# A fused Mamba and soft mixture-of-experts kernel: tables that place the second output projection, the x_proj product, both silus, GpSimd's w products and ScalarE's convolution inputs

## The chip, the cores and the metric

The kernel runs on one core of one Trainium2 chip. The metric is the device time of one execution in microseconds (us). The kernel before takes 7782.45 us, the median of three runs (7781.32 to 7786.65).

## The reference, cut to what matters

The input is one sequence of 8192 rows of width 512. It goes through a two-layer Mamba block with a residual, and then through a soft mixture of experts with a residual. The change touches the Mamba layers alone. Each of the two layers computes:

```
xz = x @ W_in.T;  xc, z = split(xz)                    # 512 -> 2 x 1024 channels
u = silu(causal_conv(xc, 4 taps) + b_c)
dt, Bm, Cm = split(u @ W_x.T, [32, 48])                # x_proj: 1024 -> 64
delta = softplus(dt @ W_dt.T + b_dt)
h_t = exp(delta_t * A) * h_{t-1} + delta_t * Bm_t * u_t   # 16 states for each of 1024 channels
y_t = sum over states of h_t * Cm_t + u_t * D
out = (y * silu(z)) @ W_out.T                          # 1024 -> 512
```

Everything is float32. The recurrence over 8192 rows cannot be cut along the sequence, so the kernel walks along it.

## The kernel before

**Tiling.** A layer is cut into 16 chunks of 512 rows; with two layers, 32 chunks run one after the other. A chunk has 128 slots: 32 groups (16 states, for each of two halves of the channels) times four blocks of 128 channels. The first half's states fill slots 0 to 63, the second half's 64 to 127. VectorE runs one scan (`h`, L1289) for two slots, so a chunk has 64 scans, at the even slots.

**What the engines do in a slot.** ScalarE computes the factor exp(delta * A) of the scan (`decay`, L928), for two slots at every even slot, and the scan reads it; the ring `decay` holds four slots, so ScalarE may run one scan ahead of VectorE. GpSimd multiplies `w` by the row of B (`bu`, L1172), one instruction for each scan, up to three scans ahead. TensorE transposes a finished state back, 128 rows at a time (`turn`, L666, one tile in every slot), and VectorE multiplies it by C and adds it up (`acc`, L1317 for the first of a half, L1319 for the others); one tile of four goes to ScalarE instead (`prod`, L958), and GpSimd adds those (`prod`, L1214, and `acc`, L1223). There are two `turn` banks, so the transposes of a slot wait until the tile of two slots before has been read. ScalarE's tiles of `prod` lie at the slots that leave 6 or 7 when divided by 8; at slots 4 and 12, and so on, VectorE's scan therefore follows the one before at once, with no `acc` between.

**The work beside the scan.** Between its transposes TensorE runs the projections of the neighbouring chunks: `conv_half` (the product with the first half of W_in), `conv` (the four taps, as products with diagonal matrices), `x_proj`, `turn_c` (C transposed), `delta` and `delta_next` (the product with W_dt), `gate` (the second half of W_in), `out` (the product with W_out) and, in the first 14 chunks of layer 0, `norm` (the transposes of the rows of the chunk after the next). Each ends in one of two `proj` banks (`RING = 2`), in turn, so a product waits until the tile two before it in the list has been taken.

**What sets the order.** The list `ORDER` names these tiles in order, and `timetable()` spreads their products over the slots by weights. ScalarE takes a finished tile `TAKE_LAG` slots after its last product, corrected by `TAKE_LATER`: it copies it out of the bank, and for `out`, `norm` and `x_proj` it issues the DMA that stores it. Within a slot ScalarE first runs the factors of the scan (at even slots), then its `prod`, then the takes. For `conv_half` a take is the copy into `conv_in` and `halo` (L815 to L818); the diagonal matrices (`taps`, L808) are made `TAPS_LEAD` slots earlier. `SILU_LATER` says how many slots after a take the silu of four blocks follows (`u`, L829, and `zy`, L871): the silu needs another table of functions, so two table loads go with it. `W_AT` and `HEAD_AT` say before which scan's input GpSimd runs the sum and the product that make the next `w` (L1154 and L1161), and the small instructions for the first column of a chunk (L1181 and L1191 to L1200).

All engines run in order and wait for each other through semaphores. After the two layers three short stages compute the mixture of experts (L1418 on); they are not touched.

Of the kernel before, what the change touches and what calls it, by code (L numbers as in the profile page):

```python
# [40 lines left out]
ORDER = [('conv_half', 0, 0), ('conv_half', 1, 0), ('delta', 4, 0), ('conv', 0, 8), ('conv_half', 2, 0), ('delta',  # L41
         5, 0), ('conv', 1, 0), ('conv_half', 3, 0), ('delta', 6, 0), ('conv', 2, 0), ('delta', 7, 0), ('conv_half',
         4, 0), ('conv', 3, 0), ('conv_half', 5, 0), ('conv', 4, 0), ('conv_half', 6, 0), ('conv', 5, 0),
         ('conv_half', 7, 0), ('conv', 6, 0), ('conv', 7, 0), ('norm', 0, 0), ('out', 0, 0), ('norm', 1, 8), ('norm', 2, 0),
         ('x_proj', 0, 0), ('norm', 3, 0), ('turn_c', 0, 0), ('out', 1, 0), ('delta_next', 0, 0),
         ('delta_next', 1, 0), ('out', 2, 0), ('delta_next', 2, 0), ('delta_next', 3, 4), ('out', 3, 0), ('gate', 0,
         4), ('gate', 1, 0), ('gate', 2, 0), ('gate', 3, 0), ('gate', 4, 0), ('gate', 5, 0), ('gate', 6, 0),
         ('gate', 7, 0)]
# [1 line left out]
SLOTS_BODY = GROUPS * HB  # L50
PAIRS = SLOTS_BODY // 2
TAKE_LAG, TAPS_LEAD, XDBL_LAG, CONV_LAG, PROD_LAG = 3, 2, 3, 3, 2
TAKE_LATER = {('out', 0): -1, ('gate', 0): 1, ('gate', 2): 2, ('delta_next', 0): -1, ('conv', 5): -1, ('delta', 5): -1}
SILU_LATER = (4, 4, 1, 1)
V_SUM_AT = (10, 10, 10, 10, 10, 10, 10, 9, 9, 9, 10, 10, 10, 10, 10, 9)
JOIN_AT = (41, 72)

W_AT = {13: ('sum', 2), 16: ('product', 2), 20: ('sum', 3), 23: ('product', 3), 47: ('sum_next', 0), 51:
        ('product_next', 0), 55: ('sum_next', 1), 59: ('product_next', 1)}

HEAD_AT = {24: ('exponent', 1), 28: ('state', 1), 56: ('exponent_next', 0), 61: ('state_next', 0)}
HEAD_EXP_AT = {51: ('exp', 1), 117: ('exp_next', 0)}
BFIRST_AT = 24

# [51 lines left out]
def timetable():  # L116
# [5 lines left out]
    for i, (kind, x, earliest) in enumerate(ORDER):  # L122
        if kind == "conv":
            earliest = max(earliest, end_of["conv_half", x] + CONV_LAG + TAKE_LATER.get(("conv_half", x), 0))
        if kind == "x_proj":
            earliest = end_of["conv", NB - 1] + TAKE_LATER.get(("conv", NB - 1), 0) + TAKE_LAG + SILU_LATER[1] + 4
        if kind in ("turn_c", "delta_next"):
            earliest = end_of["x_proj", 0] + XDBL_LAG + TAKE_LATER.get(("x_proj", 0), 0)
        slots = []
# [9 lines left out]
        end = end_of[kind, x] = slots[-1]  # L139
        late = end + TAKE_LAG + TAKE_LATER.get((kind, x), 0)  # L140
        if kind == "conv_half":
# [5 lines left out]
        if kind == "conv" and x % HB == HB - 1:  # L147
            take[late + SILU_LATER[x // HB]].append(("silu_u", x // HB, i))
        if kind == "gate" and x % HB == HB - 1:
            take[late + SILU_LATER[2 + x // HB]].append(("silu_z", x // HB, i))  # L150
    return work, take, end_of
# [142 lines left out]
def mamba_stack(nc, ctx, d, rstd, nmr):  # L294
# [828 lines left out]
    def _(pool):  # L1123
# [17 lines left out]
        def bias(X):  # L1141

            pool.wait_ge(norm_step, X * 11 + 11)
            rows = slice(X * J, X * J + J)
            pool.tensor_tensor(nmr[:, rows], neg_mean[:], rstd[:, rows], ALU.mult).then_inc(bias_set, 1)
# [91 lines left out]
        def body(G, kind):  # L1237
            for p in range(PAIRS):
                what, pair = W_AT.get(p, ("", 0))
                if what and kind.has(what.replace("sum", "delta").replace("product", "delta")):  # L1240
                    delta_w(G, what, pair)
                if p == BIAS_AT and kind.norms:
                    bias(G + NORM_AHEAD)
                if p in HEAD_AT:
                    what, hf = HEAD_AT[p]
                    X = G + what.endswith("_next")
# [906 lines left out]
```

## Time and profile before

| | |
|---|---|
| median of three runs | 7782.45 us (7781.32 to 7786.65) |
| the profiled execution | 7782.23 us, its span 7780.4 us |
| TensorE, matmuls | 7040.2 us busy, 90% of the span |
| VectorE | 7073.6 us, 91% |
| ScalarE | 6030.5 us, 78% |
| GpSimd | 6668.8 us, 86% |
| mean granted TensorE clock | 0.974 of full speed |
| VectorE's 2048 scans | the first starts 99.2 us after the span's start, the last at 7197.5 us |

A share of busy time is an average over the whole span. The two Mamba layers fill it up to the last scan; what follows belongs to the mixture of experts, in which GpSimd has little to do. In a view of the timeline, the time in brackets at the end of a row is how long the engine stood idle before that row, and what is named behind the arrow is what ended that idle time. The view of the waits adds such idle times up by pairs of waiter and releaser. PE is TensorE, DVE VectorE, ACT ScalarE, POOL GpSimd and SP the queue of DMA issues.

### The profile page before, as it was taken

The page shows a single profiled execution, that of the slowest core. Times are in us where ns is not written, and L with a number is a line of the kernel's source. Part 1 is how long each engine was busy: PE and PEld are TensorE (multiplying, and loading weights), DVE is VectorE, ACT ScalarE, POOL GpSimd, SP SyncE. Part 2 cuts the span into 40 slices and gives each one's busy share as a digit, 9 for nine tenths or more (in the row PEclk, how much of TensorE's full clock was granted, in tenths as well). Part 3 has the DMA queues.
Part 4 walks back from the last instruction along what each step waited for, and adds up shares of the span by engine and source line. Part 5 has one row for each costly group of instructions (what it writes and reads, how often), then busy time and mean ns, then how long its engine had stood idle before and what let it go on. Part 6 is the DMA issues. An engine that isn't in the chain of part 4 may idle for free. (4 is left out here: it accounts for less than half of the span.)

```text
span 7780.4 us, 98947 instructions
## 1 busy us (share of the span) xinstructions
PE 7040.2 (90%) x29580; PEld 3887.5 (50%) x29580; DVE 7073.6 (91%) x6228; ACT 6030.5 (78%) x13267; POOL 6668.8 (86%) x3115
## 2 busy tenths in 40 slices
PE   7899999999999999999999999999999999987799
PEld 3454554554454545544444445444444454444664
DVE  5999999999999999999999999999999999999655
ACT  7888888888878888877777788777777787776564
POOL 5999999999999999999999999999999999998010
PEclk9899999999999999999999999999999999998899
DMA  3222222222222222222222222222222222221665
GB/s 107 76 85 86 79 86 77 79 76 82 86 85 79 86 77 79 77 84 87 85 69 75 66 75 70 75 71 75 68 74 66 75 70 76 70 71 51 246 234 184
DMA packets 282695, 684.05 MB, mean 88 GB/s; under 512 B 37872, under 2 KB 38128, under 8 KB 254384
## 3 DMA queue, kind: packets, MB, share of 16 engines
q1 hardware_dynamic: 252464, 626.31, 24.7%
q10 hardware_dynamic: 29696, 51.40, 1.8%
q8 instruction: 239, 3.92, 0.2%
q14 instruction: 296, 2.42, 0.1%
HBM read 508.76 MB, written 168.82 MB: 87 GB/s over the span
## 5 line engine op out<-in xcount | busy, mean ns | idle before, releaser
L1172 POOL TENSOR_TENSOR bu<-w,b_rep 128x1022 f32<-128x1022 f32 x2048 | 4802.0, 2363 | 489.6 <-DVE h L1289 483.1
L1289 DVE TENSOR_TENSOR_SCAN h<-decay,bu 128x1024 f32<-128x1024 f32 x2048 | 4651.4, 2282 | 213.3 <-ACT decay L928 109.2
L666 PEld LDWEIGHTS turn<-ident_m,h 128*128 128x128 f32 x16384 | 1974.0, 143 | 2687.0 <-issue 1297.0
L928 ACT ACTIVATE decay<-delta,neg_a 128x511 f32<-128x511 f32 x4096 | 2666.4, 685 | 714.1 <-DVE h L1289 711.2
L666 PE MATMUL turn<-ident_m,h 128*128 128x128 f32 x16384 | 2573.5, 282 | 503.5 <-DVE acc L1319 465.6
L1319 DVE SCALAR_TENSOR_TENSOR acc<-turn,c_now,acc 128x512 f32<-128x512 f32 x2816 | 1972.6, 738 | 126.6 <-PE turn L666 126.2
L958 ACT ACTIVATE prod<-turn,c_now 128x512 f32<-128x512 f32 x1024 | 700.5, 684 | 504.2 <-PE turn L666 487.0
L1214 POOL TENSOR_TENSOR prod<-prod 128x1024 f32<-128x1024 f32 x448 | 1059.9, 2366 | 10.0 <-ACT prod L958 10.0
L588 PE MATMUL proj<-x_conv,w_in 128*128 128x512 f32 x2048 | 1026.2, 598 | 45.3 <-ACT halo L818 36.1
L588 PE MATMUL proj<-conv_in,conv_diag 128*128 128x512 f32 x1984 | 989.8, 598 | 68.3 <-ACT halo L818 68.3
L588 PE MATMUL proj<-x_gate,w_in 128*128 128x512 f32 x2048 | 1016.9, 596 | 0.0
L588 PE MATMUL proj<-zy,w_out 128*128 128x512 f32 x1024 | 504.5, 595 | 0.0
L588 PE MATMUL proj<-w_out,zy 128*128 128x512 f32 x1024 | 503.6, 598 | 0.9 <-DVE zy L1328 0.9
L938 ACT COPY bu<-h_first 128x2 f32<-128x2 f32 x2048 | 385.4, 188 | 51.5 <-ACT stage L877 25.5
L588 PEld LDWEIGHTS proj<-conv_in,conv_diag 128*128 128x128 f32 x1984 | 316.2, 191 | 212.3 <-ACT halo L818 108.4
L588 PEld LDWEIGHTS proj<-x_conv,w_in 128*128 128x128 f32 x2048 | 327.5, 192 | 184.0 <-issue 106.5
L588 PEld LDWEIGHTS proj<-x_gate,w_in 128*128 128x128 f32 x2048 | 327.9, 192 | 113.6 <-issue 107.4
L1154 POOL TENSOR_TENSOR delta<-delta,w 128x1024 f32<-128x1024 f32 x128 | 303.1, 2368 | 41.2 <-ACT w L862 41.2
L808 ACT ACTIVATE conv_diag<-ident_m,par 128x128 f32<-128x128 f32 x992 | 315.2, 391 | 0.4
L588 PE MATMUL proj<-u,w_x 128*64 128x512 f32 x512 | 305.6, 707 | 10.2 <-ACT u L829 10.2
L1161 POOL TENSOR_TENSOR w<-delta,u 128x1024 f32<-128x1024 f32 x128 | 303.7, 2373 | 0.3
L1317 DVE TENSOR_SCALAR acc<-turn,c_now 128x512 f32<-128x512 f32 x256 | 189.3, 741 | 106.1 <-PE turn L666 104.0
(167 smaller groups left out, 5839.9 us busy)
## 6 DMA issues: line engine op xcount, KB each, us to landing
b_rep<-b_rows SPq DMA_DIRECT2D x1024, 256.0 KB, 3.3
u_rows<-u SPq DMA_DIRECT2D x64, 1024.0 KB, 4.0
u_back<-u_rows SPq DMA_DIRECT2D x256, 256.0 KB, 3.5
x_gate<-xt SPq DMA_DIRECT2D x32, 1024.0 KB, 7.0
xt<-stage ACTq DMA_DIRECT2D x128, 256.0 KB, 2.4
x_conv<-xt SPq DMA_DIRECT2D x31, 1024.0 KB, 6.3
x_gate<-in_x_dram SPq DMA_DIRECT2D x16, 1024.0 KB, 5.3
x_l<-in_x_dram SPq DMA_DIRECT2D x16, 1024.0 KB, 10.3
```

Source lines behind the costliest of these rows:

```text
L588: mm = pe.matmul(out[0:lhs.shape[1], :], lhs, rhs, start=n == 0, stop=n == count - 1)
L666: mm = pe.transpose(out[:, b * P:(b + 1) * P], h[:, (G * GROUPS + k) % H_RING, b, j * P:(j + 1) * P], ident[:])
L808: act.activation(conv_diag[:, b % 2, k, :], ident[:], ACT.Copy, scale=par[:, STATES + k, b:b + 1])
L928: act.activation(decay[:, (G * SLOTS_BODY + s) % DEC_RING, 1:T], delta[:, blk, 1:T], ACT.Exp, scale=neg_a[:, n, blk:blk + 1]).then_inc(dec ...
L938: act.copy(bu[:, (G * PAIRS + p) % BU_RING, :, 0], h_first[:, hf, n, 2 * pr:2 * pr + 2]).then_inc(head_set, 1)
L958: act.activation(prod[:, V_BUFFER[q], k % 2, :], turn[:, BANK[tile], :], ACT.Copy, scale=c_now[:, j, n:n + 1]).then_inc(v_done, 1)
L1154: pool.tensor_tensor(delta[:, lo:lo + 2, :], delta[:, lo:lo + 2, :], w[:, lo:lo + 2, :], ALU.add).then_inc(delta_set, 1)
L1161: pool.tensor_tensor(w[:, lo:lo + 2, :], delta[:, lo:lo + 2, :], u[:, lo:lo + 2, :], ALU.mult).then_inc(w_set, 2)
L1172: pool.tensor_tensor(bu[:, (G * PAIRS + s // 2) % BU_RING, :, 1:T], w[:, blk:blk + 2, 1:T], b_rep[:, g % B_RING, 1:T].unsqueeze(1).to_broa ...
L1214: pool.tensor_tensor(total, total, prod[:, V_BUFFER[q]], ALU.add).then_inc(vsum_set, 1)
L1289: dve.tensor_tensor_scan(h[:, (G * GROUPS + k) % H_RING, 2 * pr:2 * pr + 2, :].rearrange("p b t -> p (b t)"), decay[:, at:at + 2, :].rearr ...
L1319: dve.scalar_tensor_tensor(out, src, scalar, out, ALU.mult, ALU.add).then_inc(x_done, 1)
```

## The change

In `ORDER`, `out 1` moves from behind `turn_c` to a place ahead of `x_proj`, and `norm 2` from ahead of `x_proj` to a place behind it. Every `conv_half` is taken one slot sooner, and its diagonal matrices are made one slot sooner. The silus of `u` follow two slots later than before, those of `z` three slots later after their take; the gates themselves lie two to three slots sooner, since the slots ahead of `x_proj` are filled. `turn_c` is taken a slot sooner after its product, and `delta_next 0` loses its own such correction. Six entries of `W_AT` and `HEAD_AT` move.

```
-         ('conv_half', 7, 0), ('conv', 6, 0), ('conv', 7, 0), ('norm', 0, 0), ('out', 0, 0), ('norm', 1, 8), ('norm', 2, 0),
-         ('x_proj', 0, 0), ('norm', 3, 0), ('turn_c', 0, 0), ('out', 1, 0), ('delta_next', 0, 0),
+         ('conv_half', 7, 0), ('conv', 6, 0), ('conv', 7, 0), ('norm', 0, 0), ('out', 0, 0), ('norm', 1, 8),
+         ('out', 1, 0), ('x_proj', 0, 0), ('norm', 2, 0), ('norm', 3, 0), ('turn_c', 0, 0), ('delta_next', 0, 0),
...
-TAKE_LATER = {('out', 0): -1, ('gate', 0): 1, ('gate', 2): 2, ('delta_next', 0): -1, ('conv', 5): -1, ('delta', 5): -1}
-SILU_LATER = (4, 4, 1, 1)
+TAKE_LATER = {**{('conv_half', b): -1 for b in range(8)}, ('out', 0): -1, ('gate', 0): 1, ('gate', 2): 2, ('turn_c', 0): -1, ('conv', 5): -1, ('delta', 5): -1}
+SILU_LATER = (6, 6, 4, 4)
...
-W_AT = {13: ('sum', 2), 16: ('product', 2), 20: ('sum', 3), 23: ('product', 3), 47: ('sum_next', 0), 51:
-        ('product_next', 0), 55: ('sum_next', 1), 59: ('product_next', 1)}
+W_AT = {13: ('sum', 2), 16: ('product', 2), 20: ('sum', 3), 23: ('product', 3), 46: ('sum_next', 0), 49:
+        ('product_next', 0), 52: ('sum_next', 1), 56: ('product_next', 1)}
-HEAD_AT = {24: ('exponent', 1), 28: ('state', 1), 56: ('exponent_next', 0), 61: ('state_next', 0)}
+HEAD_AT = {24: ('exponent', 1), 28: ('state', 1), 54: ('exponent_next', 0), 60: ('state_next', 0)}
```

By the timetable, in slots (before, now): `out 1` 76 to 81, now 64 to 70; `x_proj` 68 to 73, now 71 to 77; `norm 2` and `norm 3` 64 and 74, now both 77; `turn_c` 76, now 80; the last product of `gate 7` 126, now 123. ScalarE takes `x_proj` at 76, now 80; the silus of `u` stand at 40 and 64, now 42 and 66; those of `z` at 113 and 2 (of the next chunk), now 114 and 2. The four moved GpSimd instructions of the next chunk's `w` stand before the inputs of scans 47, 51, 55 and 59 of the chunk's 64 (counted from 0), now 46, 49, 52 and 56. VectorE's order does not change.

TensorE around slot 64, in the second chunk of layer 0 (`zy,w_out` is `out`, `ident_m,x_gate` is `norm`, `u,w_x` is `x_proj`). Before:

```order
L588 MATMUL proj<-zy,w_out 128x512 x2
L666 MATMUL turn<-ident_m,h 128x128 x4
L694 MATMUL proj<-ident_m,x_gate 128x128 x8
L666 MATMUL turn<-ident_m,h 128x128 x16
L588 MATMUL proj<-u,w_x 64x512 x2
L666 MATMUL turn<-ident_m,h 128x128 x4
L588 MATMUL proj<-u,w_x 64x512
L666 MATMUL turn<-ident_m,h 128x128 x4
```

Now, from the same last products of `out 0`:

```order
L588 MATMUL proj<-zy,w_out 128x512 x2
L666 MATMUL turn<-ident_m,h 128x128 x4
L694 MATMUL proj<-ident_m,x_gate 128x128 x4
L588 MATMUL proj<-zy,w_out 128x512
L666 MATMUL turn<-ident_m,h 128x128 x4
L588 MATMUL proj<-zy,w_out 128x512
L666 MATMUL turn<-ident_m,h 128x128 x4
L588 MATMUL proj<-zy,w_out 128x512
```

The row of 16 transposes is that of slots 65 to 68, and `x_proj` began behind it: two `norm` tiles and three slots without a product of their own stood between `out 0` and `x_proj`. Now one `norm` tile stands there, and the eight products of `out 1`, with a slot's transposes between them; `x_proj` begins behind these.

ScalarE at slots 64 to 68 in the same chunk (L829 is the silu of `u`, with a table load ahead and one behind; L877 takes `out 0`; L918 takes a `norm`). Before:

```order
L928 ACTIVATE decay<-delta,neg_a 128x511 x2
L969 COPY h_last<-h 128x4
L829 ACT_TABLE_LOAD
L829 ACTIVATE u<-u 128x2048
L772 ACT_TABLE_LOAD
L877 COPY stage<-proj 128x512
L879 DMA xt<-stage 128x512
L938 COPY bu<-h_first 128x2
L928 ACTIVATE decay<-delta,neg_a 128x511 x2
L918 COPY conv_in<-proj 128x512
L920 DMA xt<-conv_in 128x512
L918 COPY conv_in<-proj 128x512
```

Now:

```order
L928 ACTIVATE decay<-delta,neg_a 128x511 x2
L969 COPY h_last<-h 128x4
L877 COPY stage<-proj 128x512
L879 DMA xt<-stage 128x512
L938 COPY bu<-h_first 128x2
L928 ACTIVATE decay<-delta,neg_a 128x511 x2
L829 ACT_TABLE_LOAD
L829 ACTIVATE u<-u 128x2048
L772 ACT_TABLE_LOAD
L918 COPY conv_in<-proj 128x512
L920 DMA xt<-conv_in 128x512
L938 COPY bu<-h_first 128x2
```

The take of `out 0` stood behind the silu and ahead of the factors of scan 66; now it comes first, then these factors, and the silu stands between the factors of scans 66 and 68, with one `norm` taken behind it.

## Rows read from the trace of the kernel before

**Rows 1.** Two whole chunks: length, engine busy (instructions), clock, DMA.

```profile
2322.40:2545.00 222.60, 204.14 (x870) 110.80 (x869) 209.53 (x169) 183.85 (x411) 207.03 (x98) 0.99 0.25 81
...
4541.30:4763.00 221.70, 203.44 (x853) 109.53 (x853) 209.24 (x169) 174.34 (x384) 206.71 (x97) 0.98 0.22 72
```

**Rows 2.** Waits, layer-1 chunk: us in total, times, longest.

```profile
DVE h L1289 <- ACT decay L928: 4.3, 3, 2.2
...
DVE acc L1317 <- PE turn L666: 4.0, 4, 2.4
...
PE proj L588 <- ACT halo L818: 2.9, 4, 1.1
...
DVE acc L1319 <- PE turn L666: 2.3, 5, 1.0
...
DVE h L1289 <- POOL bu L1172: 1.6, 2, 1.1
```

**Rows 3.** Waits of VectorE, layer-0 chunk.

```profile
DVE acc L1319 <- PE turn L666: 5.6, 7, 2.2
DVE acc L1317 <- PE turn L666: 3.0, 4, 1.4
```

**Rows 4.** Timeline, VectorE, layer-1 chunk: start, us, line, idle before.

```profile
4557.69 0.75 DVE L1317 TENSOR_SCALAR acc<-turn,c_now 128x512 f32<-128x512 f32 x1 [0.35 <-PE turn L666]
...
4655.11 2.29 DVE L1289 TENSOR_TENSOR_SCAN h<-decay,bu 128x1024 f32<-128x1024 f32 x1 [2.15 <-ACT decay L928]
...
4658.62 4.46 DVE L1289 TENSOR_TENSOR_SCAN h<-decay,bu 128x1024 f32<-128x1024 f32 x2
...
4665.46 0.75 DVE L1317 TENSOR_SCALAR acc<-turn,c_now 128x512 f32<-128x512 f32 x1 [2.38 <-PE turn L666]
```

**Rows 5.** Timeline, TensorE, same chunk, slots 63 to 70.

```profile
4648.42 1.88 PE L588 MATMUL proj<-w_out,zy 128*128 128x512 f32 x4
...
4658.10 1.11 PE L666 MATMUL turn<-ident_m,h 128*128 128x128 f32 x4 [4.43 <-DVE acc L1319]
...
4659.14 3.68 PE L588 MATMUL proj<-u,w_x 128*64 128x512 f32 x4
...
4663.76 1.07 PE L588 MATMUL proj<-u,w_x 128*64 128x512 f32 x2
```

**Rows 6.** Busy time and granted clock, same chunk, slots 68 and 69.

```profile
4658.00:4663.00 5.00, 4.90 (x9) 1.72 (x10) 5.00 (x4) 1.42 (x3) 3.92 (x2) 0.50 0.03 9
```

**Rows 7.** Timeline, ScalarE, same chunk, slots 64 to 66.

```profile
4648.13 1.28 ACT L829 ACT_TABLE_LOAD   x1
...
4652.65 0.59 ACT L877 COPY stage<-proj 128x512 f32<-128x512 f32 x1
...
4653.73 1.29 ACT L928 ACTIVATE decay<-delta,neg_a 128x511 f32<-128x511 f32 x2
```

**Rows 8.** Timeline, another layer-0 chunk: VectorE, TensorE, ScalarE.

```profile
1768.07 0.75 DVE L1319 SCALAR_TENSOR_TENSOR acc<-turn,c_now,acc 128x512 f32<-128x512 f32 x1 [2.21 <-PE turn L666]
...
1766.94 0.66 PE L694 MATMUL proj<-ident_m,x_gate 128*128 128x128 f32 x4 [2.11 <-ACT stage L877]
...
1784.75 0.58 ACT L837 COPY xdbl<-proj 64x512 f32<-64x512 f32 x1 [0.63 <-PE proj L588]
...
1786.20 0.16 ACT L843 COPY spare_m<-proj 128x1 f32<-128x1 f32 x1 [0.87 <-ACT xdbl L837]
```

**Rows 9.** Timeline, GpSimd and VectorE, layer-1 chunk, slots 90 to 112.

```profile
4690.64 2.36 POOL L1172 TENSOR_TENSOR bu<-w,b_rep 128x1022 f32<-128x1022 f32 x1 [1.08 <-DVE h L1289]
...
4697.58 2.38 POOL L1154 TENSOR_TENSOR delta<-delta,w 128x1024 f32<-128x1024 f32 x1
...
4699.90 9.34 POOL L1172 TENSOR_TENSOR bu<-w,b_rep 128x1022 f32<-128x1022 f32 x4
...
4729.97 0.40 POOL L1181 TENSOR_TENSOR a_first<-neg_a,delta 128x64 f32<-128x64 f32 x1
...
4697.45 2.29 DVE L1289 TENSOR_TENSOR_SCAN h<-decay,bu 128x1024 f32<-128x1024 f32 x1
```

## The prediction

> **What bounds the kernel now.** I read the page first, then the busy time of whole chunks, then the waits in them, then the timelines of the engines around the longest waits. The reader is to see four things.
>
> First, VectorE sets the pace of a chunk: it is busy for 209.24 of 221.70 us in a chunk of layer 1 and 209.53 of 222.60 in one of layer 0, more than any other engine [rows 1]. Its instructions do not change, so all that can be won or lost is its idle time, 12.5 us and 13.1 us a chunk.
>
> Second, that idle time has a few owners. In layer 1 it is 4.3 us waiting for ScalarE's factors, 4.0 and 2.3 us for TensorE's transposes, 1.6 us for GpSimd's inputs [rows 2]; in layer 0 the transposes cost 5.6 and 3.0 us [rows 3].
>
> Third, one of these chains runs through the clock. In layer 1 scan 66 waits 2.15 us for its factors [rows 4], since ScalarE runs the silu of u ahead of them: from 4648.13 to 4652.65, 4.52 us with both table loads, and then the take of out 0, 1.08 us until the factors start [rows 7]. TensorE has no products in these slots; it stands idle for 4.43 us, and then x_proj's first two products take 3.68 us, 1.84 each, where one takes 1.07 us a little later [rows 5]. From 4658 to 4663 us the granted clock is 0.50, the lower level, 1.2 GHz [rows 6]. The transposes queue behind x_proj, and VectorE waits 2.38 us [rows 4].
>
> Fourth, where the norm tiles exist (14 chunks of layer 0), TensorE instead stands 2.11 us before norm 2, whose bank is freed by the take of out 0 behind the silu, and VectorE waits 2.21 us for it [rows 8].
>
> **The change part by part.** No instruction is added or removed; all is order. I work out each chunk's idle time of VectorE, with 17 chunks without norms (2 of layer 0, 15 of layer 1) and 14 with; the last chunk has no next one and is left out.
>
> *x_proj at half clock.* Its slots 65 to 70 now hold out 1, so TensorE has products through the silu and x_proj starts at slot 71 at full clock. Of the 4.0 us of waits in four, 0.35 us lies at slot 9 [rows 2, 4]; the rest, 3.65 us, goes: at 1.07 us a product and 0.66 us for a slot's transposes, 1.7 us, TensorE keeps up with VectorE's 3.5 us for two slots (4655.11 to 4658.62) [rows 4]. In chunks with norms 3.0 less 0.35 is 2.65 us [rows 3]. If the clock fell all the same, none of it would go.
>
> *The silu of u at slot 66.* It now stands between the factors of scans 66 and 68. The take of out 0 comes first and can't start before TensorE's last product, 4648.42 + 1.88 = 4650.30 [rows 5]; with 1.08 for the take and 1.29 for the factors [rows 7] scan 66's are ready at 4652.67, in time for the 4652.96 (4655.11 less 2.15) at which the scan could have started. The silu then runs to 4657.2, scan 68's factors to 4658.6. VectorE wants them at 4652.96 + 0.3 (below) + 3.5 = 4656.8: a wait of 1.9 us at scan 68 in place of 2.15 at scan 66. It ranges from 0, if out 0 is ready sooner, to 4.5, the whole silu. With norms a take of norm 1 (its copy and DMA issue are those of out 0, 1.0 us) stands behind the silu: 2.9 us there, and the 2.21 us before norm 2 go.
>
> *Out 1's first product* needs the bank of out 0, free 0.59 us after 4650.30, while the transposes ahead of it take about 0.3 less: 0.3 us. It is 0.6 at most, 0 at least.
>
> *Norm 3 behind x_proj* (14 chunks). It needs x_proj's own bank, which ScalarE frees at slot 80, behind the factors of scan 80, which wait for the end of scan 76. From there: 1.4 us for the factors, 1784.75 to 1786.36 or 1.6 us for the take, 0.66 for norm 3, 0.6 for the transposes of slot 78 [rows 7, 8], together 4.2 us. VectorE wants slot 78 after scan 78, which follows scan 76 with nothing between, 2.2 us (4.46 less 2.28) [rows 4]. So a new wait of 2.0 us; 0 if x_proj is taken early, 4.2 if nothing covers it. What is queued behind norm 3 on TensorE is the transposes that VectorE waits for, so this one is on the path.
>
> *Convolution inputs one slot sooner.* TensorE waits for ScalarE's halo copies four times, 2.9 us [rows 2]. Two of the eight, at slots 5 and 33, move to the end of the even slot before and stand where they stood among ScalarE's instructions; the one at 15 passes one `prod` alone. At slot 22 the take now stands ahead of the factors of scan 24, not behind, 1.4 us sooner; of VectorE's waits, the longest of the five (1.0 us) [rows 2] goes for 0.8, and 1.0 us in layer 0, where six waits share 3.4 us (5.6 less 2.21). Bounds: 0 and 2.3 us. In slots 2 to 18 I take nothing: from the silu of z at slot 2 on ScalarE runs without a gap, the same instructions in another order. If that cover is gone, the tap matrices ahead of scan 6's factors cost about the 1.3 us of a pair of factors, and the 0.35 at slot 9 is won.
>
> *The other silus.* Scan 66 owns 2.15 of the 4.3 us in three waits [rows 2, 4]; the other two share 2.15, behind the silu of u at slot 40 and that of z at 113. At 42 the silu has the take of conv 4 and the tap matrices behind it before the factors of scan 44: about 1.0 us stays. At 114 the factors of scan 114 come before the silu and those of scan 116 have two full scans' time: gone. Together -1.15, between 0 and -2.15.
>
> *GpSimd's next w.* At scan 45 its input is ready 4.45 us early (4690.64 + 2.36 against 4697.45) [rows 9]. Each large instruction takes 2.31 us from start to start (9.34 us for four) [rows 9], the first column's 0.40; VectorE takes 3.5 us a scan, 2.2 at every fourth. Counting the lead from scan 45, with sums before 46, 51 and 55 and the moved ones before 46, 49, 52, 56: 4.45 + 3.5 - 6.95 = 1.0 at scan 46, then 0.9, 2.1, 0.9 at 49, 2.1, and 2.1 + 2.2 - 4.65 = -0.35 at 51: a wait. At 52 0 + 3.5 - 4.65, 1.15; then leads of 1.2 and 2.0, at 55 -0.45, at 56 1.15 again. In sum 3.1 to 3.2 us against 1.6 now [rows 2]: +1.6. The ends are -1.6 (all hidden) and +7.7, all four moved instructions exposed (9.3 less 1.6). I take +1.6, since the recurrence rests on these rows.
>
> *The sum.* Without norms: -3.65 - 2.15 + 1.9 + 0.3 - 0.8 - 1.15 + 1.6 = -3.95 us, times 17 = -67. With norms: -2.65 - 2.21 + 2.9 + 0.3 + 2.0 - 1.0 - 1.15 + 1.6 = -0.2, times 14 = -3. Together -70 us from the profiled execution's 7782.2 us, which stands 0.2 us under the median of the three runs: 7712 us.
>
> On SP's queue the store of u waits for the later silus, and the load of x_gate at slot 88 for the take of norm 3, now at 80; gate 0 reads it at 96. Behind the store stands the next row of B, and GpSimd, 4.45 us ahead or more, hides such a delay; I count nothing.
>
> **The rivals.**
> *The hole has moved (slower).* gate 7 now ends at slot 123, so slots 125 to 127 have transposes alone, as slots 65 to 67 had. If the clock falls there in every chunk at the old price, 3.65 and 2.65 us, then 17 x 3.65 + 14 x 2.65 = 99 us come back: 7712 + 99 = 7811. For it: a stretch from 4650.30 to 4659.14 with transposes alone preceded the fall [rows 5, 6]. Against it: the 4.43 us of idleness in that stretch came from the late scan, and no scan is late at slot 126; the new stretch is about half as long, and ScalarE has the say in the slots behind it. It decides from 70 / 31 = 2.3 us a chunk. The Trainium skill (TensorE: Matmul & The Clock Gate, section "Part 4: PE-mode transpose") says that transposes do not count as busy for the clock in the way that matmuls do. By that rule slots 125 to 127 count as idle whatever stands in them, and the time goes towards this rival's; the rows agree with it, and with plain idleness as well.
>
> *More is won.* If norm 3's wait and the silu's at 68 were hidden by half, 14 x 2.5 + 17 x 1 = 52 us more go: 7660. For it: my bounds for both reach to 0. Against it: both follow from the order of ScalarE alone.
>
> *The waits only change places.* ScalarE's bursts keep their lengths, so each silu finds a scan to hold up, GpSimd takes back what the clock gives, and the time stays within 0.2%, 7767 to 7798. For it: in my own sum two of the three silus' waits come back, 1.9 and 1.0 us. Against: the x_proj term stands apart from them.
>
> *GpSimd binds (slower).* With its four instructions all exposed, 6.1 us more a chunk than I took, 31 x 6.1 = 189 us: 7901. Against: the recurrence.
>
> **How the numbers follow.** I give 0.60 to the forecast (its own range 7675 to 7760), 0.14 to more won, 0.09 to no change, 0.12 to the moved hole and 0.05 to GpSimd. About 0.2% is what a measurement of this kernel can tell from none. Faster is then 0.60 + 0.14 = 0.74; same 0.09; slower 0.12 + 0.05 = 0.17. The range reaches from 7650 to 7800 us and leaves out the ends of the two outer rivals.
>
> **What would show it.** Right: the low clock before x_proj is gone and its products take 1.07 us throughout; VectorE's longest wait is for the factors of scan 68; in chunks with norms a wait for transposes of about 2 us at slot 78; GpSimd's waits double to about 3 us in four; chunks of layer 1 last 218 us, those of layer 0 stay near 222.5. Wrong: the low clock shows up around slot 0, a wait for inputs above 5 us a chunk, or a wait at slot 68 near 4.5 us.

## The result, and the profile after

The changed kernel takes 7742.22 us, the median of four runs (7739.22 to 7746.63); the kernel before took 7783.26 us in its four runs beside them (7781.32 to 7786.65). The ratio is 0.9947, with a 95% interval of 0.9930 to 0.9964: it is faster, by 41 us where 70 were forecast. The profiled execution took 7740.15 us, its span 7738.3 us, at a mean granted clock of 0.976 (0.974 before).

The first view is again two whole chunks, the first of layer 0 and the second of layer 1: length, then the busy time (instructions) of TensorE, its weight loads, VectorE, ScalarE and GpSimd, the clock and the DMA share.

```profile
2338.88:2564.19 225.31, 207.44 (x870) 113.29 (x869) 209.62 (x169) 184.15 (x411) 207.12 (x98) 0.98 0.25 80
4543.15:4761.78 218.63, 202.29 (x855) 108.89 (x854) 208.96 (x170) 174.39 (x384) 206.67 (x97) 0.99 0.23 73
```

VectorE is busy as long as before [rows 1]; its idle time fell by 2.8 us in layer 1 and rose by 2.6 us in layer 0. Its waits in that layer-1 chunk (in total, times, longest):

```profile
DVE h L1289 <- PE turn L666: 3.3, 2, 2.3
DVE h L1289 <- ACT decay L928: 3.1, 3, 1.1
DVE acc L1319 <- PE turn L666: 2.2, 4, 1.4
...
DVE h L1289 <- POOL bu L1172: 0.8, 2, 0.5
```

The group of 4.0 us at L1317, `x_proj`'s price in layer 1 [rows 2], is gone. The two waits in the first row are not TensorE's: scan 68 stands there with 2.3 us, and its factors came 0.09 us before it started; scan 104 stands there with 1.0 us, and its input from GpSimd came last. In the second row scan 112 stands with 1.0 us, and its input came last too. So GpSimd has four waits with 2.8 us in all, as forecast (3.1 to 3.2), and not the two of the last row. The clock and the order of work show the gain plainly. First busy time and granted clock of the five us in which `x_proj` starts, then the timelines of TensorE, ScalarE and VectorE around slots 66 to 70:

```profile
4662.00:4667.00 5.00, 3.80 (x15) 1.65 (x14) 5.00 (x5) 4.60 (x11) 3.36 (x2) 1.00 0.41 95
```
```profile
4665.14 1.93 PE L588 MATMUL proj<-u,w_x 128*64 128x512 f32 x4
```
```profile
4653.96 1.30 ACT L928 ACTIVATE decay<-delta,neg_a 128x511 f32<-128x511 f32 x2
4655.27 1.28 ACT L829 ACT_TABLE_LOAD   x1
4656.57 1.91 ACT L829 ACTIVATE u<-u 128x2048 f32<-128x2048 f32 x1
4658.50 1.28 ACT L772 ACT_TABLE_LOAD   x1
...
4659.89 1.29 ACT L928 ACTIVATE decay<-delta,neg_a 128x511 f32<-128x511 f32 x2
```
```profile
4661.27 4.47 DVE L1289 TENSOR_TENSOR_SCAN h<-decay,bu 128x1024 f32<-128x1024 f32 x2 [2.28 <-PE turn L666]
```

The first four records of `x_proj` take 1.93 us, where they took 3.68 [rows 5], at a granted clock of 1.00, the level of 2.4 GHz, where it was 0.50 [rows 6]. The silu stands between the factors of scans 66 and 68, and scan 68 waits 2.28 us (1.9 were forecast).

Not all that went there was the clock's. In chunks 4 and 12 of the kernel before (layer 0) the low stretch ended before `x_proj`, whose first four records took 1.93 us; VectorE waited 0.70 and then 0.44 us for transposes all the same. TensorE, then VectorE, in chunk 4 of the kernel before:

```profile
1105.44 1.93 PE L588 MATMUL proj<-u,w_x 128*64 128x512 f32 x4
```
```profile
1111.17 0.75 DVE L1317 TENSOR_SCALAR acc<-turn,c_now 128x512 f32<-128x512 f32 x1 [0.70 <-PE turn L666]
```

What was not forecast lies elsewhere. In the layer-1 chunk, at slots 44 to 47: ScalarE, TensorE, VectorE, and the clock.

```profile
4611.72 1.91 ACT L829 ACTIVATE u<-u 128x2048 f32<-128x2048 f32 x1
4613.65 1.28 ACT L772 ACT_TABLE_LOAD   x1
4614.95 0.69 ACT L825 ACTIVATE u<-proj,par 128x512 f32<-128x512 f32 x1
4615.53 1.26 ACT L808 ACTIVATE conv_diag<-ident_m,par 128x128 f32<-128x128 f32 x4
...
4616.79 1.30 ACT L928 ACTIVATE decay<-delta,neg_a 128x511 f32<-128x511 f32 x2
...
4618.20 0.57 ACT L816 COPY conv_in<-proj 128x512 f32<-128x512 f32 x1
...
4620.20 0.67 ACT L958 ACTIVATE prod<-turn,c_now 128x512 f32<-128x512 f32 x1
```
```profile
4620.92 0.66 PE L666 MATMUL turn<-ident_m,h 128*128 128x128 f32 x4 [2.15 <-ACT prod L958]
4621.42 1.47 PE L588 MATMUL proj<-conv_in,conv_diag 128*128 128x512 f32 x2
4622.68 1.06 PE L666 MATMUL turn<-ident_m,h 128*128 128x128 f32 x4
4623.53 1.89 PE L588 MATMUL proj<-conv_in,conv_diag 128*128 128x512 f32 x2
```
```profile
4618.17 2.29 DVE L1289 TENSOR_TENSOR_SCAN h<-decay,bu 128x1024 f32<-128x1024 f32 x1 [1.02 <-ACT decay L928]
...
4623.78 0.75 DVE L1319 SCALAR_TENSOR_TENSOR acc<-turn,c_now,acc 128x512 f32<-128x512 f32 x1 [0.54 <-PE turn L666]
4625.90 0.75 DVE L1319 SCALAR_TENSOR_TENSOR acc<-turn,c_now,acc 128x512 f32<-128x512 f32 x1 [1.37 <-PE turn L666]
```
```profile
4621.80:4625.20 3.40, 3.40 (x8) 1.63 (x7) 2.19 (x2) 3.20 (x8) 3.40 (x3) 0.51 0.12 39
```

Behind the silu ScalarE takes `conv 4`, makes the tap matrices of block 6 and takes `conv_half 6`. Its `prod` of slot 46 is then so late that TensorE idles 2.15 us for the bank; the clock falls to 0.51, the lower level of 1.2 GHz, and two records of `conv 5` take 1.89 us instead of 1.02. VectorE pays 0.54 + 1.37 us. In the kernel before, neither engine waited there (the same transposes, then VectorE's reads):

```profile
4619.28 0.65 PE L666 MATMUL turn<-ident_m,h 128*128 128x128 f32 x4
```
```profile
4622.72 1.39 DVE L1319 SCALAR_TENSOR_TENSOR acc<-turn,c_now,acc 128x512 f32<-128x512 f32 x2
```

In chunk 17 the same idle time of 2.15 us is followed by a clock of 1.00, and VectorE waits only 0.33 us. So most of the price at slot 46 is paid only where the clock falls:

```profile
3966.79 0.66 PE L666 MATMUL turn<-ident_m,h 128*128 128x128 f32 x4 [2.15 <-ACT prod L958]
...
3968.58 1.02 PE L588 MATMUL proj<-conv_in,conv_diag 128*128 128x512 f32 x2
```
```profile
3967.20:3971.00 3.80, 3.80 (x20) 2.21 (x19) 3.47 (x4) 3.38 (x8) 3.80 (x3) 1.00 0.20 70
```
```profile
3970.08 0.75 DVE L1319 SCALAR_TENSOR_TENSOR acc<-turn,c_now,acc 128x512 f32<-128x512 f32 x1 [0.33 <-PE turn L666]
```

In layer 0 the same kind of fall stands at slot 26 (before `conv_half 4`, whose bank ScalarE frees late) in eight of the chunks 1 to 13, and at slot 78 (norm 3) in seven of them. One chunk's timeline of TensorE, then of VectorE, each with slot 26 first and slot 78 behind it, and then busy time and clock of both stretches:

```profile
1710.09 1.92 PE L588 MATMUL proj<-x_conv,w_in 128*128 128x512 f32 x2 [1.26 <-ACT u L825]
...
1802.63 1.12 PE L694 MATMUL proj<-ident_m,x_gate 128*128 128x128 f32 x4 [2.10 <-ACT spare_m L843]
1803.54 2.75 PE L666 MATMUL turn<-ident_m,h 128*128 128x128 f32 x12
```
```profile
1712.90 0.75 DVE L1319 SCALAR_TENSOR_TENSOR acc<-turn,c_now,acc 128x512 f32<-128x512 f32 x1 [2.15 <-PE turn L666]
...
1804.63 1.60 DVE L1319 SCALAR_TENSOR_TENSOR acc<-turn,c_now,acc 128x512 f32<-128x512 f32 x2 [2.96 <-PE turn L666]
```
```profile
1709.00:1714.00 5.00, 3.91 (x8) 2.00 (x9) 2.85 (x4) 3.28 (x8) 5.00 (x3) 0.66 0.15 52
...
1802.00:1806.00 4.00, 3.37 (x15) 2.98 (x16) 1.26 (x2) 2.45 (x6) 4.00 (x2) 0.57 0.72 156
```

The Trainium skill (TensorE: Matmul & The Clock Gate, section "A second HAM failure mode: psum-queue depth-cycling") describes TensorE losing its clock to short idle times while it cycles through banks; the rows at slots 26, 46 and 78 agree, with idle times of 1.26, 2.15 and 2.10 us before a bank, though chunk 17 has the same 2.15 us and no fall. The prediction had looked for the fall at slot 126 only.

**Where the time went, by slot.** The interval from one scan's start to the next one's, as a mean over 13 chunks of each layer (1 to 13 of layer 0, 17 to 29, all of layer 1), after less before, in us a chunk, gathered under the prediction's steps:

| step | forecast, layer 1 / layer 0 with norms | measured |
|---|---|---|
| `x_proj` at half clock (slots 70, 72) | -3.65 / -2.65 | -3.94 / -2.63 |
| silu of u at 66 and out 1's first product (slots 64, 66) | +0.05 / +0.99 | +0.10 / +0.91 |
| norm 3 (slot 78) | 0 / +2.0 | -0.35 / +2.42 |
| convolution inputs, slots 4 to 22 | -0.8 / -1.0 | -1.19 / -1.35 |
| the same, slots 26 to 30 and 46 | 0 / 0 | +1.77 / +2.48 |
| other silus (slots 40, 42, 112) | -1.15 / -1.15 | -1.20 / -1.20 |
| GpSimd's next w (slots 100 to 110) | +1.6 / +1.6 | +1.34 / +1.34 |
| sum | -3.95 / -0.2 | -3.47 / +1.97 |

### The profile page after: what moved, and what is told of

It is laid out like the page before. It is cut to its first block and busy times, and to the rows that moved or that the text cites. A ratio compares the mean times of both kernels' runs of the same rounds, so it can differ in the third digit from the quotient of the medians.

```text
span 7738.3 us, 98947 instructions
## 1 busy us (share of the span) xinstructions
PE 7041.3 (91%) x29580; PEld 3889.1 (50%) x29580; DVE 7067.0 (91%) x6228; ACT 6032.2 (78%) x13267; POOL 6666.9 (86%) x3115
## 3 DMA queue, kind: packets, MB, share of 16 engines
q8 instruction: 239, 3.92, 0.2%
q14 instruction: 296, 2.42, 0.1%
## 5 line engine op out<-in xcount | busy, mean ns | idle before, releaser
L588 PE MATMUL proj<-x_conv,w_in 128*128 128x512 f32 x2048 | 1052.1, 611 | 18.1 <-ACT u L825 17.0
L674 PE MATMUL turn<-u_back,d_diag 128*128 128x512 f32 x512 | 284.0, 637 | 2.6 <-issue 1.1
L588 PE MATMUL proj<-u,w_x 128*64 128x512 f32 x512 | 271.4, 625 | 10.4 <-ACT u L829 10.4
```

Source lines behind the costliest of these rows:

```text
L588: mm = pe.matmul(out[0:lhs.shape[1], :], lhs, rhs, start=n == 0, stop=n == count - 1)
```

## The experiments

Each time is the median of four to eleven runs, taken beside the kernel before; the ratio is to that kernel. What is said of slots comes from each kernel's one profiled execution.

**The order alone.** The kernel before with the new `ORDER`; of the corrections only `turn_c`'s moves in place of `delta_next`'s, and the silus of z stay in their slots.

```
-TAKE_LATER = {... ('delta_next', 0): -1, ...}
-SILU_LATER = (4, 4, 1, 1)
+TAKE_LATER = {... ('turn_c', 0): -1, ...}
+SILU_LATER = (4, 4, 3, 4)
```

> The kernel before with the new ORDER alone: out 1 ahead of x_proj, norm 2 and 3 behind it; silus, takes of the convolution inputs and GpSimd's w at their old slots (the silus of z are corrected so that they stay at 113 and 2). Theory A (out 1 keeps TensorE in products, so x_proj runs at full clock; each silu still holds up one scan): in layer 1 the 3.65 us behind x_proj go, but out 1's first product waits for the take of out 0, which stands behind the silu of u, and VectorE waits 2.6 us at slot 65 in place of 2.15 at scan 66: -3.2 us a chunk; with norms -2.65 - 2.21 + 2.6 + 3.0 (norm 3 behind x_proj) = +0.7: 7783 - 17 x 3.2 + 14 x 0.7 = 7738. Rival B (moving out 1 only pays with the silu behind it): TensorE's idle time of about 2.7 us before out 1 lowers the clock there as it did before x_proj, 1.8 us more a chunk: 7783 and up.

Measured: 7738.6 us, ratio 0.9942 (0.9930 to 0.9955). The interval of slot 70 shrinks by 3.07 us in layer 1 and 2.09 in layer 0, and that of slot 78 grows by 2.43 in layer 0. So the new order by itself gives as much as the whole change, as theory A had it (7738), and everything else in the change sums to about nothing. Two things differ from the changed kernel. The 0.5 us of slot 72 stays, so that part of the gain needs the rest of the change. And with the silu still ahead of `out 1`, the clock falls at slots 64 or 66 in 12 of the chunks 1 to 30, as rival B had it, where the changed kernel has no fall at these slots; in the five of them in layer 1 slot 70 takes about 5.0 us instead of 3.5.

**The convolution inputs taken as before.** The changed kernel without the entries of `conv_half`.

```
-TAKE_LATER = {**{('conv_half', b): -1 for b in range(8)}, ('out', 0): -1, ...}
+TAKE_LATER = {('out', 0): -1, ...}
```

> The changed kernel with every convolution input taken at its old slot; all else as changed. Theory A (the earlier takes cost more than they give: they put copies and tap matrices ahead of the factors at slots 6, 44 and of prod 46, TensorE stands idle 2.15 us at slot 46 and the clock falls behind it): in layer 1 the wait at slot 44 (1.0) and those of slot 46 (1.8) go, the one at slot 22 comes back (0.9), slots 4 to 18 stay the same in sum: -2.0 us a chunk; with norms -1.1 -0.8 -1.4 (slot 26) -0.3 + 1.35 = -2.2: 7742 - 17 x 2.0 - 14 x 2.2 = 7677. Rival C (the earlier takes are where the change gains): slower than 7742, towards 7765, as the 2.9 us a chunk that TensorE waited for the halo copies come back.

Measured: 7706.57 us (7697.6 to 7712.8), ratio 0.9899 (0.9886 to 0.9913). Undoing the earlier takes makes the changed kernel 36 us faster: the sign of this step was wrong. The falls at slots 26 and 46 are gone, the interval of slot 42 shrinks by 1.10 us in both layers, that of slot 46 by 1.29 in layer 1, that of slot 26 by 1.42 in layer 0; slot 22 takes back 0.92 and 1.35. The direction is theory A's, the size a little over half of the 65 us expected.

**Norm 3 behind turn_c.** The changed kernel, with norm 3 no longer next in line for `x_proj`'s bank.

```
-         ('x_proj', 0, 0), ('norm', 2, 0), ('norm', 3, 0), ('turn_c', 0, 0),
+         ('x_proj', 0, 0), ('norm', 2, 0), ('turn_c', 0, 0), ('norm', 3, 0),
-TAKE_LATER = {... ('turn_c', 0): -1, ...}
+TAKE_LATER = {... ('turn_c', 0): -2, ...}
```

> The changed kernel with norm 3 behind turn_c, so that its bank is norm 2's and not x_proj's, and turn_c taken one more slot sooner. Theory A (norm 3 waits 2.1 us for x_proj's bank, with the transposes of slot 78 behind it, and the clock that falls there makes it 2.96 us of VectorE's time): -2.7 us in each of 14 chunks, 7742 - 38 = 7704. Rival B (the wait is that for the take of x_proj itself, which turn_c needs anyway): it comes back at slot 80, and the time stays within 6 us of 7742.

Measured: 7707.92 us (7705.22 to 7711.37), ratio 0.9902 (0.9888 to 0.9915). Slot 78 shrinks by 2.78 us in layer 0, and 0.74 comes back at slot 86; another 0.80 goes at slots 100 and 102, and layer 1 hardly changes (+0.13). Norm 3's wait was on the path, as forecast.

**A product ahead of the transposes at slot 46.** An attempt to take the fall of the clock away by order alone.

```
+                if s not in WORK_FIRST:      # WORK_FIRST = (46,)
+                    transposes(s)
                 for what, x, i, lo, hi in WORK[s]:
...
+                if s in WORK_FIRST:
+                    transposes(s)
```

> The changed kernel with one difference: at slot 46 TensorE issues conv 5's product ahead of the slot's transposes, so that a product stands inside the 2.15 us in which it waits for ScalarE's prod 46. No wait is taken away. Theory A (VectorE's wait of 1.9 us at slots 46 and 47 is the price of the clock that falls behind this idle time, not of the wait for the bank): the clock stays up at slot 46, layer-1 chunks last 216.9 us as the chunks without the fall do, 13 chunks x 1.7 and about 8 of layer 0 x 1: 7742 - 30 = 7712. Rival B (the wait for the bank itself is what VectorE pays): the transposes still start when prod 46 is done, and the time stays at 7742 within 5 us.

Measured: 7737.59 us (7733.74 to 7744.21), ratio 0.9939 (0.9926 to 0.9953): no change that can be told. TensorE and VectorE at slots 44 to 47 of the same chunk (the line numbers stand one to seven higher in this kernel):

```profile
4624.32 0.84 PE L667 MATMUL turn<-ident_m,h 128*128 128x128 f32 x4 [2.16 <-ACT prod L965]
4624.95 3.43 PE L589 MATMUL proj<-conv_in,conv_diag 128*128 128x512 f32 x4
```
```profile
4628.86 1.41 DVE L1326 SCALAR_TENSOR_TENSOR acc<-turn,c_now,acc 128x512 f32<-128x512 f32 x2 [2.23 <-PE turn L667]
```

The product did not get into the hole: the idle time is 2.16 us as before. The transposes that wait for `prod` are those of slot 45, and the edit moved the product ahead of the transposes of slot 46, behind the hole. The clock falls in 13 of the chunks 14 to 30, as it did, and the wait of VectorE only becomes one piece. So the run tests neither theory; what a filled hole would do is not known.

**conv_half 6 alone put back.**

```
-TAKE_LATER = {**{('conv_half', b): -1 for b in range(8)}, ...}
+TAKE_LATER = {**{('conv_half', b): -1 for b in (0, 1, 2, 3, 4, 5, 7)}, ...}
```

> The changed kernel with conv_half 6 and its tap matrices alone put back where they were before. Theory A, the early take of conv_half 6 piles ScalarE's work up behind the silu of u, and that makes both the wait of scan 44 and TensorE's idle time of 2.15 us ahead of slot 46, behind which the clock falls: the waits after slots 42 and 46 shrink by 1.1 and 1.3 us in layer 1, by 1.1 and 0.3 us in layer 0, the low clock at slot 46 goes, 16 x 2.3 + 13 x 1.35 = 54 us, 7688 us (7678 to 7700). Theory B, the silu at slot 42 makes the hole whatever stands behind it, and the clock falls all the same: only the 1.1 us at slot 42 goes, 29 x 1.1 = 32 us, 7710 us or more.

Measured: 7676.83 us (7674.72 to 7680.61), ratio 0.9864 (0.9851 to 0.9878): theory A, 1 us below its lower bound. One take and its four matrices cost 65 us. Slots 44 to 47 of the same chunk, TensorE, then VectorE:

```profile
4577.95 0.66 PE L666 MATMUL turn<-ident_m,h 128*128 128x128 f32 x4 [1.39 <-ACT prod L958]
...
4579.74 1.02 PE L588 MATMUL proj<-conv_in,conv_diag 128*128 128x512 f32 x2
```
```profile
4578.08 2.29 DVE L1289 TENSOR_TENSOR_SCAN h<-decay,bu 128x1024 f32<-128x1024 f32 x1 [0.36 <-POOL bu L1172]
...
4581.24 0.75 DVE L1319 SCALAR_TENSOR_TENSOR acc<-turn,c_now,acc 128x512 f32<-128x512 f32 x1 [0.23 <-PE turn L666]
```

The idle time is 1.39 us instead of 2.15, the clock does not fall, and scan 44's wait of 1.02 us is gone too. A full chunk of layer 1 takes 216.1 us instead of 218.6. The falls at slot 26 went as well, in all layer-0 chunks but one (eight before). That was not expected, and why is not settled; slots 26 and 78, where the clock fell less often, hold about 13 of the 65 us.

**The convolution inputs alone, on the kernel before.**

```
-TAKE_LATER = {('out', 0): -1, ...}
+TAKE_LATER = {**{('conv_half', b): -1 for b in range(8)}, ('out', 0): -1, ...}
```

> The kernel before with one edit alone: every conv_half and its tap matrices one slot sooner. Theory A, what these takes cost in the changed kernel comes from their meeting the silu of u at slot 42; with that silu at slot 40 there is no pile at slots 42 to 46, slot 22 gains 0.9 us in layer 1 and 1.35 in layer 0, where slot 26 takes about as much back, and slots 4 to 14 change nothing: 7784 - 15 = 7769 us (7755 to 7778). Theory B, the takes cost the same 36 us by themselves, wherever the silu stands: about 7820 us. By the prediction's own term they give 0.8 and 1.0 us a chunk, 28 us: 7756 us.

Measured: 7770.27 us (7757.62 to 7775.01), ratio 0.9982 (0.9973 to 0.9991): theory A. With the silu of u at slot 40, slot 22 shrinks by 0.92 us in layer 1 and 1.35 in layer 0, slot 26 takes 0.86 back in layer 0, slot 40 grows by 0.28, and slots 42 to 46 do not change. So the takes are worth 13 us alone and cost 36 in the changed kernel: together with the run before, this puts the price on their meeting the silu at slot 42. A part of the gain is the clock's, since slot 70 shrank by 0.46 us in layer 1; the profiled execution is also the fastest of the eleven, 12.7 us below their median.

**Norm 3 behind turn_c, and of the convolution inputs conv_half 3 alone sooner.** The changed kernel with both edits.

```
+         ('x_proj', 0, 0), ('norm', 2, 0), ('turn_c', 0, 0), ('norm', 3, 0),
+TAKE_LATER = {('conv_half', 3): -1, ('out', 0): -1, ... ('turn_c', 0): -2, ...}
```

> The changed kernel with the convolution inputs taken as before, except conv_half 3, which stays one slot sooner, and with norm 3 behind turn_c. Theory A, the costs are separate waits at separate slots: layer 1 gains what the old takes gave (1.1 us a chunk) and keeps the 0.9 us of slot 22, 16 chunks x 2.0 = 33 us; layer 0 gains 1.8 + 1.35 for the takes and 2.5 for norm 3, 13 x 5.7 = 74 us; 7742 - 107 = 7635 us, between 7620 and 7655. Theory B, the gains overlap, since each shortens the same idle time of VectorE or moves a clock fall elsewhere: about 7675 us.

Measured: 7652.69 us (7650.81 to 7655.45), ratio 0.9832 (0.9818 to 0.9845): nearer to theory A, at the edge of its range. Norm 3's and slot 22's gains come whole. Slot 26 in layer 0 stays at 4.53 us where the clock stays up and takes 5.5 to 5.9 where it falls, against 3.85 us in the kernel before and in the one with all takes as before: that loss belongs to conv_half 3. What is missing lies in falls of the clock at slot 26 in six layer-0 chunks, and at slot 8 in five chunks.

**GpSimd's old places in the changed kernel.** `W_AT` and `HEAD_AT` as before.

```
-W_AT = {... 46: ('sum_next', 0), 49: ('product_next', 0), 52: ('sum_next', 1), 56: ('product_next', 1)}
-HEAD_AT = {... 54: ('exponent_next', 0), 60: ('state_next', 0)}
+W_AT = {... 47: ('sum_next', 0), 51: ('product_next', 0), 55: ('sum_next', 1), 59: ('product_next', 1)}
+HEAD_AT = {... 56: ('exponent_next', 0), 61: ('state_next', 0)}
```

> The changed kernel with the old places of GpSimd's sums, products and first-column instructions. Theory A, the recurrence over GpSimd's instructions: with VectorE free of its other waits, the old places would make it wait about 2.9 us a chunk, the new ones do so for 2.8 us; the time stays at 7742 us within 8. Theory B, the move itself makes the extra wait of 1.2 us a chunk (1.6 us before, 2.8 us now): undoing it gives 31 x 1.2 = 37 us, 7705 us.

Measured: 7722.66 us, ratio 0.9923 (0.9910 to 0.9937), between the two theories. Slots 102 and 110 shrink by 1.11 us each, 108 takes 0.81 back and 116 0.93: 0.48 us a chunk, 15 us of the 20. The old places wait at scan 118 once the silu of z no longer holds scan 114 up. The rest are fewer falls of the clock in layer 0.

**GpSimd's new places alone, on the kernel before** (the same edit the other way round).

> The kernel before with one edit alone: the new places of GpSimd's sums, products and first-column instructions. By the recurrence over GpSimd's rows of the kernel before, scans 104 and 112 wait 1.1 us each, scan 110 gets 0.8 us back, and the wait of scan 114 for its factors shrinks by 0.3: 1.1 us a chunk, 31 x 1.1 = 34 us, 7783 + 34 = 7817 us (7805 to 7828). If the move costs only what its undoing gave in the changed kernel, 0.48 us a chunk, it is 7798 us. If GpSimd's instructions were hidden, 7783 us.

Measured: 7797.47 us (7796.08 to 7802.19), ratio 1.0018 (1.0009 to 1.0027). The slots came as the recurrence has them (102 and 110 +1.11 each, 108 -0.83, 112 -0.29: +1.1 us), and yet the time is that of the smaller claim. In layer 1 slot 70 shrank by 1.00 us. `x_proj`, VectorE's wait behind it, and the new wait of scan 104, whose input from GpSimd came late:

```profile
4672.31 3.06 PE L588 MATMUL proj<-u,w_x 128*64 128x512 f32 x4
```
```profile
4677.59 0.75 DVE L1317 TENSOR_SCALAR acc<-turn,c_now 128x512 f32<-128x512 f32 x1 [1.35 <-PE turn L666]
...
4733.13 2.29 DVE L1289 TENSOR_TENSOR_SCAN h<-decay,bu 128x1024 f32<-128x1024 f32 x1 [1.02 <-PE turn L666]
```

The low stretch begins 113.4 us after the chunk's first scan, where it began at 115.6; fewer of `x_proj`'s records fall into it (3.06 us against 3.68), and VectorE waits 1.35 us instead of 2.38 [rows 4, 5]. A delay 35 slots later in the chunk gave back most of what it cost, through the clock.

**All three repairs.** conv_half 6 as before, norm 3 behind `turn_c`, GpSimd's old places.

```
+         ('x_proj', 0, 0), ('norm', 2, 0), ('turn_c', 0, 0), ('norm', 3, 0),
+TAKE_LATER = {**{('conv_half', b): -1 for b in (0, 1, 2, 3, 4, 5, 7)}, ... ('turn_c', 0): -2, ...}
+W_AT = {... 47: ('sum_next', 0), 51: ('product_next', 0), 55: ('sum_next', 1), 59: ('product_next', 1)}
+HEAD_AT = {... 56: ('exponent_next', 0), 61: ('state_next', 0)}
```

> The changed kernel with what the runs so far point to: conv_half 6 and its tap matrices back where they were, norm 3 behind turn_c, and GpSimd's old places. If the three are separate waits, the gains add up: 7676.8 us for the first, 2.5 us in each of 13 chunks less for norm 3, and 0.48 us in each of 31 chunks less for GpSimd's places: 7676.8 - 32.5 - 15 = 7629 us, between 7615 and 7645. If they overlap, or a fall of the clock takes another place, it stays above 7650 us.

Measured: 7634.05 us (7631.07 to 7637.62), ratio 0.9806 (0.9793 to 0.9819), within 5 us of the sum of the three. It beats both kernels, by 108 us the changed one. The same two chunks as at the top of this part:

```profile
2290.18:2509.28 219.10, 202.69 (x869) 110.42 (x868) 209.19 (x169) 183.62 (x411) 206.87 (x98) 1.00 0.27 82
4464.11:4679.78 215.67, 200.26 (x854) 108.14 (x853) 208.74 (x169) 174.36 (x384) 206.51 (x97) 1.00 0.24 74
```

VectorE's work is the same, its idle time 9.9 and 6.9 us, and the clock is 1.00 in both.

## Why the prediction was right, and where its sum was off

**Right in sign and in its main steps.** The waits behind `x_proj` were the one large gain, -3.94 and -2.63 us a chunk against -3.65 and -2.65, and the order alone shows that most of it comes from the new `ORDER`. The prediction put all of it down to the half clock, and that is too much: where `x_proj` ran at full clock in the kernel before (chunk 4), 1.14 us of waits stood there all the same, so in layer 0 the clock had about 1.5 us of the 2.65. That the whole went is in part luck. For layer 1 no run separates the two. The silu's wait did move from scan 66 to scan 68 at nearly the forecast price (2.28 us, forecast 1.9; 2.89 in layer 0, forecast 2.9). GpSimd's recurrence came within 0.3 us a chunk. The other silus did too (-1.20, forecast -1.15), but that is luck: the row holds 1.09 us at slot 42 that goes with conv_half 6, and without it the silus gave -2.29, beyond the bound of -2.15.

**The step that failed: convolution inputs one slot sooner.** The prediction gave it -0.8 and -1.0 us, and measured were +0.58 us in layer 1 and +1.13 in layer 0 beside the wait at scan 44; undone, it gives 36 us. Five of the eight takes (those at slots 8, 24, 40, 46 and 54) now stand ahead of a pair of factors instead of behind one. The prediction worked out the one at 24 alone, set the early slots at nothing, and said nothing of 40, 46 and 54. It treated slot 22 rightly and priced the tap matrices ahead of scan 6 (slot 4 +1.14, paid back at slots 8 to 14), but not the same move at slot 44. There the matrices (1.26 us) and the take (0.85 us with its three copies) come on top of the silu, the `prod` of slot 46 gets late, TensorE's bank stays full, and the clock falls in 13 of the 17 chunks 14 to 30. In layer 0 slots 26 and 28 have the larger part, 1.56 of 2.48 us: conv_half 3, taken sooner, won 1.35 us at slot 22, and at slot 26 0.68 us of it comes back, or about 1.9 us where the clock falls. The prediction had that wait of 1.0 us at scan 44 right, but booked it under the silu as something that stays, where it goes with conv_half 6; and it did not follow the chain one engine further, to TensorE. For slots 2 to 18 it named what the move costs if ScalarE has no slack; for the later slots its bounds, 0 to 2.3 us of gain, excluded a loss without a reason.

**Norm 3's size.** Against the 3.48 us without it, the interval of slot 78 is 2.19 us longer in the layer-0 chunks whose clock stays up and 3.26 in most where it falls, 2.78 in the mean, against 2.0 forecast. The prediction priced norm 3 and the transposes behind it at 0.66 and 0.6 us; after 2.10 us of idleness norm 3 takes 1.12 where the clock falls.

**The rivals.** *The hole has moved* named a real effect: the clock does fall near slot 126, in 18 chunks. It costs nothing there: the interval of scan 126 is 3.50 us in all 31 chunks, fallen or not, and the two intervals behind it (slots 0 and 2 of chunks 1 to 30) add up to 7.3 us either way. The rival's mechanism came true at other slots instead, 26, 46 and 78, where TensorE idled for a bank with VectorE one slot behind it. *More is won* gave a time that the repaired kernel reaches, 7634 us, by another way: norm 3's wait goes, but the one at scan 68 stays, and slot 46 and GpSimd's old places give the rest. *The waits only change places* describes layer 0, whose chunks got 2 us longer, but not layer 1, and the time lies outside its range. *GpSimd binds* is refuted by the slots 100 to 110.

**Open.** Why the clock falls at slot 26 or 46 in one chunk and not in the next with the same idle time (2.15 us in chunks 17 and 20 at slot 46, 1.26 us in chunks 4 and 7 at slot 26) was not found out. The silus' moves were not run alone: that the hole at slot 46 needs the silu at slot 42 is concluded from the run of the convolution inputs alone, which lacks the rest of the change too.

## What to carry to other kernels

When an instruction is moved ahead on a busy in-order engine, add up everything that then stands between two deadlines of that engine, at every place where the move repeats, and follow the late one to the next engine; a table that moves eight takes alike hits eight different neighbourhoods. An idle time of TensorE is priced by what follows it: behind the wait for a bank at slot 46 two records took 1.89 us instead of 1.02 where the clock fell, so look for new holes in every slot where a producer gets later, and ask whether a reader stands right behind. Test the parts one by one: here the part that cost was worth 13 us alone.

## What was not expected of the hardware

The granted clock falls behind idle times of TensorE as short as 1.26 us (slot 26, 0.66 over 5 us) and yet stays up behind 2.15 us in chunk 17. In these traces a fall costs what its readers feel: nothing at slot 126, 1.7 us of an interval at slot 46 (median 5.61 us against 3.92 without a fall), 1.2 us at slot 26 (5.75 against 4.53). And the place of a low stretch within a chunk moves with unrelated delays, which is worth 1.0 us a chunk in the run with GpSimd's places alone.
